# Edge indices loaded a pass ahead, padding tiles left out, and W3 Wp folded in a four-block graph network

## The reference

```python
h = gat_conv(h, ei, W3, as3, ad3, b3, 1, OUT_DIM)
h = h @ Wp + bp
nrm = jnp.linalg.norm(h, axis=-1, keepdims=True)
return h / jnp.maximum(nrm, 1e-12)
```

## Time and profile before

| what | value |
|---|---|
| median of 3 executions | 15680.2 us (15678.73 to 15681.94) |
| the profiled execution, its span | 15693.26 us, 15691.1 us |
| mean granted TensorE clock | 0.696 |
| busy: PE, DVE, ACT, POOL | 52%, 42%, 36%, 72% of the span |
| GpSimd's gathers of eg1 to eg3 (4992) and of e0 and e3 (3328), busy | 4720.5 and 3157.4 us |

### The profile page before, as it was taken

The page is one execution under the profiler, slowest core; times in us unless marked ns, Lnnn a source line. Parts: engine busy times, 40 slices in busy tenths (PEclk is TensorE's granted clock), DMA queues, the critical chain, the costliest instruction groups (busy, mean ns, idle before and its releaser), DMA issues. The chain is left out here.

```text
span 15691.1 us, 260578 instructions
## 1 busy us (share of the span) xinstructions
PE 8152.2 (52%) x75456; PEld 7432.0 (47%) x75456; DVE 6592.3 (42%) x23913; ACT 5724.4 (36%) x13579; POOL 11298.3 (72%) x11964
## 2 busy tenths in 40 slices
PE   6555552565564963434432344341444444888886
PEld 4455551455554853333322333331444443777776
DVE  5555554677775962333344333335222224211112
ACT  2555551677774832222211222220112112333332
POOL 4777776677777777777767777766777774677776
PEclk9777775778886966666665666665555555899998
DMA  4444442222222934444433444443333332444443
GB/s 153 162 162 162 160 151 63 95 91 91 91 94 99 344 126 127 145 146 148 143 110 86 144 148 144 147 134 58 81 84 86 83 86 53 126 144 146 148 144 103
DMA packets 885671, 1964.80 MB, mean 125 GB/s; under 512 B 383207, under 2 KB 461555, under 8 KB 844368
## 3 DMA queue, kind: packets, MB, share of 16 engines
q0 software_dynamic: 357792, 578.42, 16.7%
q1 hardware_dynamic: 435263, 856.32, 16.1%
q10 hardware_dynamic: 92320, 527.01, 8.5%
HBM read 1095.68 MB, written 894.33 MB: 127 GB/s over the span
## 5 line engine op out<-in xcount | busy, mean ns | idle before, releaser
L112 POOL DMA_INDIRECT eg_got<-gat_table,eg_rows x4992 | 4720.5, 946 | 1541.3 <-issue 1515.4
L112 POOL DMA_INDIRECT e_got<-table,e_rows x3328 | 3157.4, 949 | 1032.6 <-issue 1003.6
L1368 ACT ACTIVATE eg_outs<-eg_ps_sum 128x544 f32<-128x544 f32 (+1 forms) x1248 | 676.5, 542 | 4284.5 <-PE eg_ps_sum L1361 4270.5
L1361 PE MATMUL eg_ps_sum<-eg_got,eg_equal 128*128 128x136 f32 (+1 forms) x9984 | 2077.3, 383 | 272.9 <-DVE eg_got L1449 254.3
L1361 PEld LDWEIGHTS eg_ps_sum<-eg_got,eg_equal 128*128 128x128 f32 x9984 | 1972.4, 291 | 336.1 <-ACT eg_outs L1368 181.0
L117 POOL DMA_INDIRECT sorted_rows<-sort_rows,sort_dest x1664 | 1617.2, 972 | 533.1 <-issue 500.2
L1393 PE MATMUL eg_small<-ident,eg_score 128*128 128x128 f32 (+1 forms) x312 | 138.4, 443 | 3176.9 <-DVE eg_score L1432 3176.9
L1393 PEld LDWEIGHTS eg_small<-ident,eg_score 128*128 128x128 f32 (+1 forms) x312 | 47.2, 151 | 3204.3 <-DVE eg_score L1432 3204.3
L1430 DVE TENSOR_TENSOR eg_diff<-eg_small,eg_got 128x128 f32<-128x128 f32 (+1 forms) x312 | 79.0, 253 | 2737.5 <-DMA eg_got<-gat_table,eg_rows 2737.5
L1661 DVE TENSOR_SCALAR e_got<-e_ps_second 128x512 f32<-128x512 f32 x416 | 287.7, 692 | 1760.7 <-PE e_ps_second L1644 1721.1
L582 PE MATMUL e_ps_sum<-e_got,e_equal 128*128 128x64 f32 x3328 | 628.3, 352 | 669.0 <-DMA e_got<-table,e_rows 669.0
(11 more groups left out here) (517 smaller groups left out, 20951.7 us busy)
## 6 DMA issues: line engine op xcount, KB each, us to landing
gat_out<-eg_outs ACTq DMA_DIRECT2D x208, 1152.0 KB
eg_equal_b<-equal_d SPq DMA_DIRECT2D x312, 512.0 KB
out<-e_outs ACTq DMA_DIRECT2D x104, 1024.0 KB
values<-e_zeros_b SPq DMA_DIRECT2D x104, 768.0 KB
values_q<-e_zeros_b SPq DMA_DIRECT2D x104, 768.0 KB
sort_value<-values_q SPq DMA_DIRECT2D x104, 768.0 KB
e_value<-values SPq DMA_DIRECT2D x104, 768.0 KB
eg_got<-gat_table,eg_rows POOLq DMA_INDIRECT x4992
```

What stands on the lines that cost most here:

```text
L112: return e.indirect_dma_start(out, None, table, bass.IndirectOffsetOnAxis(ap=index, axis=0), **kw)
L1361: last_i = e.matmul(ps_sum[q % 2][:, i, 0:FG], equal[q % 4][:, i, :], got[k][:, t, :], start=True, stop=True)
L1368: e.activation(outs[k % 2][:, tiles, 0:FG], ps_sum[q % 2][:, :, 0:FG], ACT.Copy).then_inc(copied.sem, 1)
```

## The change

- `edge_rows`: the index tiles are allocated once for the whole kernel. At the end of e0, eg1, eg2 and eg3, SyncE loads the first four groups' indices again, so that the next pass finds them; e0 loads its own first four first of all. The primes of the gather counters go, and in e0, eg and e3 ScalarE's primes become plain increments.
- `REAL`: the last turn is written out behind the loop (25 turns), and its last group has 13 tiles instead of 16. The users wait for `arrived`, 48 less. In the sort the last 3 tiles of places are written by one plain transfer.
- The carried pass loads its tile keys behind its first four loads instead of at its end.
- g1c and g2c have two buffers for `own_rows`, the first two loaded at the start.
- W3 Wp: g2c opens the third layer with a weight of 64 + 64 columns, W3 and W3 Wp (made by one matmul from a transposed load of W3 and a load of Wp). The logits come from the first half, in PSUM; the table gets the second. g3c has no lin_p; its bias is b3 Wp + bp, made by one matmul. W1a's bias b1a moves into e3's first ReLU, and in g3c ScalarE instead of VectorE copies lin_a's products out.

The core of the diff (the changes of e0 and e3 are like those shown for the attention pass):

```diff
+def arrived(gathered, it, k):
+
+    buf, turn = k % len(G4), k // len(G4)
+    missing = GT - REAL[buf] if isinstance(it, int) and it + turn == TURNS - 1 else 0
+    return gathered[buf].at(it, 1 + turn) - 16 * missing
...
+            def load(g, k):
+                e.dma_start(rows[k][:, :, :], source[g, :, :, :].rearrange("g p t c -> (g p) t c")).then_inc(loaded[k].sem, 16)
...
+                load(bass.ds(k, 1), k)
...
+            for k in G4:
+                e.wait_ge(split.sem, split.at(TURNS - 1, k + 1))
+                e.wait_ge(keyed.sem, keyed.at(TURNS - 1, k + 1))
+                e.wait_ge(gathered[k].sem, arrived(gathered, TURNS - 1, k))
+                e.dma_start(rows[k][:, :, :], source[k, :, :, :]).then_inc(again, 16)
...
+                for t in range(tiles):
+                    if t and t % QT == 0:
+                        e.wait_ge(look_read.sem, look_read.at(it, (k + 1) * QUADS + t // QT - 2))
+                        e.sem_inc(turns, 1)
+                    scatter(e, self.sorted_rows, dest[k][:, t:t + 1], rows[k][:, t, :]).then_inc(moved[k].sem, 16)
+                if tiles < GT:
+                    e.dma_start(by_group(self.sorted_rows)[it * n4 + k, :, tiles:, :], rows[k][:, tiles:, :]).then_inc(tail_moved, 16)
...
             for k in G4:
                 load(0, k)
+            keys.load(e)
...
-            keys.load(e)
...
+            for k in G4:
+                e.sem_inc(rows_in[k].sem, 16)
+            for k in G4:
+                bring_value(bass.ds(k, 1), k)
+                bring_equal(bass.ds(k, 1), k)
+            with e.Fori(0, TURNS - 1) as it:
                 for k in G4:
-                    g = bass.ds(it * len(G4) + k, 1)
-                    e.wait_ge(cuts.sem, cuts.at(it, 5 * (k + 1 - n4)))
-                    e.dma_start(value[k][:, :, :], values_v[g, :, :, :].rearrange("g p t c -> (g p) t c")).then_inc(loaded[k].sem, 16)
-                    e.wait_ge(gathered[k].sem, gathered[k].at(it, 0))
-                    e.dma_start(rows[k][:, :, :], source[g, :, :, :].rearrange("g p t c -> (g p) t c")).then_inc(loaded[k].sem, 16)
-                    e.wait_ge(equaled.sem, equaled.at(it, (k + 1) * QUADS - U))
-                    e.dma_start(equal_b[k][:, :, :], equal_v[g, :, :, :].rearrange("g p t c -> (g p) t c")).then_inc(brought[k].sem, 16)
+                    g = bass.ds(it * len(G4) + (len(G4) + k), 1)
+                    e.wait_ge(cuts.sem, cuts.at(it, 5 * (k + 1)))
+                    bring_value(g, k)
+                    e.wait_ge(gathered[k].sem, gathered[k].at(it, 1))
+                    e.dma_start(rows[k][:, :, :], source[g, :, :, :].rearrange("g p t c -> (g p) t c")).then_inc(rows_in[k].sem, 16)
+                    e.wait_ge(equaled.sem, equaled.at(it, (k + 1) * QUADS))
+                    bring_equal(g, k)
...
+            for k in G4:
+                e.wait_ge(keyed.sem, keyed.at(TURNS - 1, k + 1))
+                e.wait_ge(gathered[k].sem, arrived(gathered, TURNS - 1, k))
+                e.dma_start(rows[k][:, :, :], source[k, :, :, :]).then_inc(again, 16)
+            e.wait_ge(again, 4 * 16)
...
+            def group(it, k, tiles):
+                e.wait_ge(rows_in[k].sem, rows_in[k].at(it, 1))
+                for t in range(tiles):
+                    if t % QT == 0:
+                        e.wait_ge(summed.sem, summed.at(it, (k + 1) * QUADS - U + t // QT))
+                        e.sem_inc(turns, 1)
+                    gather(e, got[k][:, t, :], table[:, :], rows[k][:, t, 1:2]).then_inc(gathered[k].sem, 16)
+
+            with e.Fori(0, TURNS - 1) as it:
+                for k in G4:
+                    group(it, k, GT)
             for k in G4:
-                e.dma_start(ph.prime(), self.ident[0:16, 0:1]).then_inc(gathered[k].sem, 16)
-            with e.Fori(0, TURNS) as it:
-                for k in G4:
-                    e.wait_ge(loaded[k].sem, loaded[k].at(it, 1))
-                    for t in range(GT):
-                        if t % QT == 0:
-                            e.wait_ge(summed.sem, summed.at(it, (k + 1) * QUADS - U + t // QT))
-                            e.sem_inc(turns, 1)
-                        gather(e, got[k][:, t, :], table[:, :], rows[k][:, t, 1:2]).then_inc(gathered[k].sem, 16)
+                group(TURNS - 1, k, REAL[k])
 
         def dve_key(e, it, k):
+            e.wait_ge(rows_in[buf(k)].sem, rows_in[buf(k)].at(it, 1 + k // len(G4)))
...
             opened.sync_weights(e)
-            close.sync_small(e)
-            for j in range(n_chunks + 1):
-                if j < n_chunks:
-                    close.sync_rows(e, j)
-                if j:
-                    opened.sync_store(e, j - 1)
+            close.sync_first(e)
+            for j in range(n_chunks):
+                if j + close.ring < n_chunks:
+                    close.sync_rows(e, j + close.ring)
+                opened.sync_store(e, j)
...
+            if after is not None:
+                opened.join_weights(e)
...
         def scalar(e):
-            def normed(j):
-                lin_p.scalar(e, j)
-                lin_p.done(e, j)
-                e.activation(sq[:, :, :], y[:, CHUNKS[j], :], ACT.Square).then_inc(squared, 1)
-                e.wait_ge(measured, j + 1)
-                e.activation(root[:, :], length[:, :], ACT.Sqrt).then_inc(rooted, 1)
-                norm.scalar(e, j)
-            in_steps(lambda j: close.merge.scalar(e), normed, lambda j: lin_a.scalar(e, j))
+            def project(e, b, ts, n, ps):
+                j = ts.start // CHUNK
+                at = slice(ts.start - CHUNKS[j].start, ts.stop - CHUNKS[j].start)
+                e.activation(hid[j % 2][:, at, :], ps, ACT.Copy).then_inc(lin_a.out, 1)
+
+            for j in range(n_chunks + 1):
+                if j < n_chunks:
+                    close.merge.scalar(e)
+                if j:
+                    if j >= 3:
+                        e.wait_ge(hid_out[(j - 1) % 2], (j - 1) // 2 * 16)
+                    lin_a.scalar_through(e, j - 1, project, slice(0, 3))
+                if j < n_chunks:
+                    e.wait_ge(closed, j + 1)
+                    e.activation(sq[:, :, :], y[:, CHUNKS[j], :], ACT.Square).then_inc(squared, 1)
+                if j:
+                    lin_a.scalar_through(e, j - 1, project, slice(3, 4))
+                if j < n_chunks:
+                    e.wait_ge(measured, j + 1)
+                    e.activation(root[:, :], length[:, :], ACT.Sqrt).then_inc(rooted, 1)
+                if j:
+                    lin_a.scalar_through(e, j - 1, project, slice(4, None))
+                if j < n_chunks:
+                    norm.scalar(e, j)
...
+    def tensor(self, e):
+        e.wait_ge(self.w_in, 48)
+        if self.after is not None:
+            e.wait_ge(self.after_in, 32)
+            e.matmul(self.ps_w[:, 0:self.HF], self.w_t[:, :], self.w_after[:, :], start=True, stop=True).then_inc(self.joined, 1)
+            e.wait_ge(self.w_made, 1)
+
+    def join_weights(self, e):
+        e.wait_ge(self.joined, 1)
+        e.tensor_copy(self.w[:, self.kept_at:], self.ps_w[:, 0:self.HF]).then_inc(self.w_made, 1)
...
+    def scalar_through(self, e, j, evacuate, some=slice(0, None)):
+        def out(b, ts):
+            e.wait_ge(self.made, b + 1)
+            n = ts.stop - ts.start
+            evacuate(e, b, ts, n, self.ps_o[b % self.n_o][:, 0:n, :])
+        todo = list(self.batches(j))
+        for i in list(range(len(todo) + 1))[some]:
+            if i < len(todo):
+                self.scalar(e, j, slice(i, i + 1))
+            if i:
+                out(*todo[i - 1])
...
+    def add_bias(self, e, more):
+        e.wait_ge(self.small_in, 32)
+        e.tensor_tensor(self.bias[:, :], self.bias[:, :], more, ALU.add).then_inc(self.ve, 1)
+        e.wait_ge(self.ve, self.c(1))
...
-            hid, hh = self.hid(j)[:, at, :], self.hid(j)[:, at, 0:HF]
+            hid = self.hid(j)[:, at, :]
+            h = ps[:, :, 0:HF] if self.after is not None else hid[:, :, 0:HF]
             s_prod, d_prod = self.tmp[0][:, 0:k, :], self.tmp[1][:, 0:k, :]
-            e.tensor_copy(hh, ps[:, :, :]).then_inc(out, 1)
+            e.tensor_copy(hid[:, :, 0:HF], ps[:, :, self.kept_at:]).then_inc(out, 1)
             e.wait_ge(out, 5 * b + 1)
-            e.tensor_tensor(s_prod, hh, across(self.a_src[:, :], k), ALU.mult).then_inc(out, 1)
+            e.tensor_tensor(s_prod, h, across(self.a_src[:, :], k), ALU.mult).then_inc(out, 1)
```

259 lines of the change are left out of this document (145 added, 114 removed).

## The result

The changed kernel takes 15498.78 us (median, 15493.59 to 15499.77), the kernel before on the same chip 15679.47 us (15673.76 to 15681.94): a ratio of 0.9885 with the interval 0.9867 to 0.9902, or 180.7 us less. Forecast were 177.5 us less and 15503 us. The total came out; several terms did not, and their errors cancelled. That is what the rest is about.

The account below looks back on a forecast made before the run. GpSimd's queue was taken to bound most long passes, DMA the carried pass and VectorE g3c. Terms 41.2 + 18.8 + 8 + 3.3 + 5 + 27.2 + 74 = 177.5 us, off the median 15680.2, gave 15503 us (15474 to 15551).

Parts of the forecast that it names:

- Rival 4: All edge passes: the gather's period grows, for example by 48 ns, costing 399 us and giving 15902 us; chance 0.03.
- Rival 3: Pass starts and tails: gathers can't start early and the late landing stays, 28 us back, 15531 us; chance 0.07.
- Pass starts: Five edge passes: no primes or index waits, 50.1 us less 3.8 in e0 and 5.1 in e3, net 41.2 us (37 to 47).
- e3's step: Start of e3: gathers move forward by 8.6 plus 2.06 us, then the 65th waits 5.1 us for TensorE's fourth quad of sums.
- Padding: Five edge passes: 3 of 1664 tiles left out of each, 15 gathers at 1.25 us, 18.8 us gained.
- The sort: Sort: 3 scatters, priced at 3.8 us, become one plain transfer of 0.5 us, 3.3 us gained.
- Tails behind the last gather: Ends of five passes: last gathers land late because their indices are alike; leaving padding out gains 8 us (0 to 11.5).
- Carried pass: e1: keys loaded first end the phase 7.6 us earlier, 2.4 us given back at the start, net 5 us (-2 to 8).
- g1c and g2c: Closings: own rows two chunks ahead remove GpSimd's waits of 22.5 and 16.4 us, net 27.2 us (0 to 36).
- the factor 0.70: Closings: GpSimd loses 0.30 us per us of VectorE beside it, so 38.9 us of removed waits give 27.2.
- Rival 1: Closings: GpSimd is held as much as it no longer waits, gain 0 to 10 us; carried pass nothing; 15530 us; chance 0.2.
- g3c: VectorE's chain there: without the Wp stage and with ScalarE copying W1a's products, 74 us less (50 to 80).

Follow-up runs that it names:

- u_preload: Changed kernel with eg1 to eg3 and e3 loading their first index tiles at the pass's start, no primes; eg2's gap before its first gather 6.52 us against 4.97.
- both_edits: Changed kernel with e3's gathers waiting only for their buffer's last reader, x's addition in 14 pieces, g3c's root ahead of the last outputs; 15481.23 us, ratio 0.9871.
- after2: The changed kernel unaltered, run again as a control; 15503.33 us against 15681.13 for the kernel before, ratio 0.9887.
- u_pad: Changed kernel with all 1664 tiles gathered and scattered, no padding left out; eg3's last packet ends 3.71 us after the last gather, against 1.95.
- no_1660: Changed kernel also leaving out tile 1660 (20 real edges, 108 padding places); eg3's last packet ends 1.64 us after the last gather, against 1.95.
- u_ring1: Changed kernel with one own-row buffer in g1c and g2c, as before; g1c takes 346.0 us and g2c 336.2, against 324.5 and 319.6.
- g3c_order: Changed kernel with ScalarE taking g3c's root before the last copy and last two outputs; six chunks take 128.1 us against 134.4.

## Why the prediction was right, and where it was not

**The kind of bound: right.** The long passes are GpSimd's queue before and after, the period of the gathers did not change, and what was taken out of the queue came off the time. Rival 4 would have shown in the first row of groups. Rival 3 would have shown in e0 and the attention passes, where gathers do start early. Nor do phases end at the index reloads; the last one of eg3 is issued beside the first use of the last gather, 18 us before SyncE's first load of the next phase (12957.50), and ScalarE's last store of the pass follows only at 12953.81:

```profile
12936.04 0.94 POOL L113 DMA_INDIRECT eg_got<-gat_table,edge_rows  x1 [0.30 <-issue]
12939.28 0.33 SPq L1393 DMA_DIRECT2D edge_rows<-pairs_d  x1
12939.29 0.18 DVE L1493 TENSOR_TENSOR eg_diff<-eg_small,eg_got 128x16 f32<-128x16 f32 x1 [8.12 <-DMA eg_got<-gat_table,edge_rows]
```

**Pass starts: 36 for 41.2 us, and e3's step failed.** e0 gave 9.9 us and the three attention passes 6.6, 9.5 and 9.1, together 35.1. The prediction had 35.6 for these (50.1 less e3's 8.6 + 2.06 and e0's 3.8): right, though its two parts were not what it took them for (u_preload). In e3 it gave 5.5 and the trace shows 1.1. The start moved forward by 10.6 us, but then:

```profile
13275.73 1.06 PE L1732 MATMUL e_ps_sum<-e_got,e_equal 128*128 128x128 f32 x8
...
13277.57 0.94 POOL L113 DMA_INDIRECT e_got<-table,edge_rows  x1 [15.66 <-PE e_ps_sum L1732]
```

The prediction took the 65th gather for the first that waits, since it is the first that reuses a buffer, and let it wait for the fourth sum. But the code asks for sums three quads earlier than its buffers do: the 65th waits for the fourth, and the 53rd already for the first. (The description of the kernel before has it wrong in the same way: a quad of `got` waits for the sums of the quad 13 before it, not 16.) With that, the trace of before gives the answer. There the first sum stood at 13465.74 for 1.06 us and the 53rd gather at 13468.47, 1.7 us behind its end; moved forward by 10.6 it is 8.9 us too early, 9.7 with the 0.8 us that it takes from the sum's end to the gather. The trace shows 5.8 us more, because the gather that the 6.68 us of `x<-x,w_bias_e` held before is held no longer: the addition now runs during the wait (from 13261.6), and 9.7 + 5.8 = 15.5 us. The 65th gather starts 95.3 us after the first, where it was 85.8. Of the 10.6 us 1.1 are left. All this goes for the granted clock of 0.50 that both traces show there. At that clock both_edits, which removes the wait and most of what the addition costs, gains 12.4 us.

**Padding: 18.8 us, right in kind and somewhat small.** Three periods of 1.25 us leave 3.75 us per pass. e0 is shorter by 2.2 us, and by 3.9 in after2; but the three attention passes are shorter by 5.8 to 6.1 us, and by 4.9 to 5.2 in after2, so always by 1 to 2 us more than the tiles left out. Where that comes from was not found out. The sort is 6.3 us shorter, 4.7 in after2, for the 3.3 forecast.

**Tails behind the last gather: 8 for 9.1 us.** From the last gather's end to the next phase's first gather, the five passes lost 1.3, 1.8, 1.0, 2.9 and 2.1 us (10.4 in all in after2). VectorE starts 2.31 us behind the last gather of eg3 instead of 3.8 (rows above): later than the 1.5 us of mid pass, as the forecast's middle value had it. The excess that is left belongs to tile 1660, whose packets land at 1.95 us instead of 1.2 to 1.3 (see u_pad and no_1660).

**Carried pass: 5 for 2 to 4 us.** The gain at the end was underestimated (8.8 for 7.6 us) and so was the loss at the start: the key transfer's 12.0 us had been put at the duration that it had at the end of the pass.

**g1c and g2c: 27.2 forecast, 39.0 measured; the term that was mis-sized.** g1c is 21.1 us shorter, g2c 17.9. The step that failed is the factor 0.70. The 0.30 us lost per us of VectorE was a mean over the gathers' window alone; used as a price for every us of VectorE's work that comes to lie beside GpSimd's, it asked for 22.5 x 0.30 = 6.8 us in g1c, where 0.4 came. For g2c the same factor held: 11.5 forecast, and 11.4 and 12.1 without the fold. But there GpSimd's busy time is cut by the fold on the other side, 5.8 to 6.5 us that the prediction had at nothing. Rival 1, which took the loss for larger than 0.30, is refuted by u_ring1. The Trainium skill, SBUF - State Buffer, section "SBUF: two separate sides", was cited against the change. The traces bear its rule out for single long instructions: 6.70 us for a gather beside 6.68 us of VectorE, 1.30 us beside pieces of 0.62. They don't for g1c as a whole.

**g3c: 74 forecast, 77.9 measured.** The row that answers the earlier trace rows:

```profile
L2924 DVE TENSOR_TENSOR g3c_e_own<-g3c_own_rows,g3c_own_dst x7: 183/185/186, 13024.1 to 13158.5; 128x14 f32<-128x14 f32 x7
```

A merge every 22.4 us (134.4/6; forecast 23.1), and from the first merge to the last copy 167.5 us instead of 245.4. The step with ScalarE came as described, a little smaller; one chunk of it:

```profile
13099.50 0.36 ACT L2699 ACTIVATE g3c_lin_a_src_t<-g3c_lin_a_ps_t 64x256 f32<-64x256 f32 x1
...
13100.39 0.60 ACT L2526 ACTIVATE g3c_hid_a<-g3c_lin_a_ps_o 128x512 f32<-128x512 f32 x1 [0.52 <-PE g3c_lin_a_ps_o L2687]
...
13101.00 1.28 ACT L2542 ACT_TABLE_LOAD   x1
...
13102.30 0.21 ACT L2542 ACTIVATE g3c_root<-g3c_length 128x14 f32<-128x14 f32 x1
...
13102.54 0.24 DVE L3124 RECIPROCAL g3c_inv_l<-g3c_root 128x14 f32<-128x14 f32 x1 [1.62 <-ACT g3c_root L2542]
```

The output at 13100.39 waits for TensorE and pushes the table load to 13101.00, and VectorE waits 1.62 us for the root. Before it waited 0.28, so 1.3 us per chunk came back where the forecast had 1.7. Over seven chunks VectorE waited 10.0 us, before 2.0. g3c_order shows that some 7 us come back if the output stands behind the root. The gathers, with 143.4 us for 98, did not become the chain.

**The sum.** 36.2 + 18.8 + 9.1 + 4.7 (the sort, by after2) + 3 + 39.0 + 77.9 = 188.7 us, against 177.5 forecast, 180.7 by the medians and 199.4 between the profiled spans. What is missing to the last is mostly the passes, which in this trace shortened by 6.8 us more than the 18.8; the rest is spread over the sort, the carried pass and block 0's closing. The forecast's nearness to the median, 4 us, is partly luck: 5 us too much at the starts and 2 in the carried pass stood against 12 too little in the closings and 4 in g3c.

## What to carry to other kernels

When a queue's start is moved forward, read from the code which instruction waits for which count, and lay that against the times of the trace; what the buffers need is only a lower bound. A mean loss per us of a neighbour's work, read over one window, is not a price for work that moves: ask which instructions make it up, for here one long one cost nearly its whole length and fourteen short ones a third of that. And price a small transfer by what stands in its queue where it will be issued, not where it stood.

## What the runs showed of the hardware

**TensorE's clock decides whether e3 of the changed kernel waits.** The same stretch of the same kernel, TensorE's own work at the start of e3 (columns as in the earlier trace rows; the granted clock is the third number from the right). In the first profiled execution:

```profile
13225.00:13240.00 15.00, 15.00 (x72) 14.29 (x71) 4.15 (x6) 3.56 (x6) 11.34 (x13) 0.50 0.21 54
```

and in after2, where the pass began 1.3 us later:

```profile
13211.00:13226.00 15.00, 15.00 (x138) 15.00 (x137) 7.61 (x11) 6.78 (x12) 11.34 (x12) 1.00 0.21 55
```

In both, TensorE had been busy for half of the last 41 us of g3c at 0.50, that is 1.2 GHz, and idle for some 6 us ahead of e3. In after2 it had 2.4 GHz within 12 us of the phase's start (0.69 over the first 12 us), in the other execution only about 60 us in (0.74 over 13255 to 13276). With it the first sum came 51.7 us after the first gather instead of 78.4, the 53rd gather found it done, and one gather was held by the addition to x instead:

```profile
13237.32 6.42 POOL L113 DMA_INDIRECT e_got<-table,edge_rows  x1 [0.30 <-issue]
```

e3 took 2080.11 us there, 8.6 less, with not a line of code changed. The traces of before and of both_edits have 0.50 there, as the first one. What makes the grant come early or late the traces do not tell.

**GpSimd and VectorE.** Whether one long VectorE instruction or fourteen short ones stand beside the gathers makes 5.8 or 1.8 us, although the short ones are the longer work (14 x 0.616 = 8.6 us). g2c's transfers became 6 us cheaper at equal VectorE time when its products began to read PSUM.

**Gathers with equal indices.** In eg3 a packet took 0.46 us in the last padding tiles, 0.19 in the tile with 108 padding places and 0.10 in mid pass.

**A small transfer behind large ones.** The key transfer needed 12.0 us at the start of the carried pass, 3.2 at its end.
